# One level of Strassen's algorithm for the base product of batch 1 in a fused cross-attention and LoRA feed-forward kernel

## The reference

```python
q1 = fake_quant(layernorm(x), x1_scale, x1_zp)      # 2 x 1024 x 2048
q2 = fake_quant(ctx, x2_scale, x2_zp)               # 2 x 2048 x 2048
x = x + q1 @ q2                                     # below: x2
n = layernorm(x)
logits = n @ W_router.T                             # 8 experts, two best, softmax weights w
h = einsum('td,erd->ter', n, lora_A)                # rank 16
lora = einsum('ter,eor,te->to', h, lora_B, w) * 2.0
x = x + n @ W_base.T + b_base + lora
```

## Time and profile before

| | |
|---|---|
| median of 3 runs | 1072.69 us (1072.56 to 1073.93) |
| the profiled execution | 1072.88 us |
| its span | 1070.9 us |
| mean granted TensorE clock | 0.99 |
| x2 stage, about | 46 to 308 us |
| routing, about | 308 to 359 us |
| base stage | 359 us to the end |
| moved by DMA | 125.48 MB |

### The profile page before, as it was taken

One profiled execution on the slowest core, in us unless ns is written; L12 is line 12 of the kernel. 1 busy time (PEld: TensorE's weight loads), 2 busy tenths in 40 slices (PEclk: granted clock), 3 DMA queues, 4 the chain that ended last, 5 costly groups with the idle time before them and its releaser, 6 DMA issues.

```text
span 1070.9 us, 15600 instructions
## 1 busy us (share of the span) xinstructions
PE 1011.0 (94%) x6039; PEld 542.3 (51%) x6039; DVE 721.6 (67%) x1334; ACT 311.5 (29%) x284; POOL 18.7 (2%) x40
## 2 busy tenths in 40 slices
PE   0497999899999999999999999999999999999997
PEld 0355666566689644444444444444444444444443
DVE  6758898688756886665665756657566584665744
ACT  3769988778641200010100100101001010010100
POOL 0000000000000000000000000000000000000000
PEclk9899999999999999999999999999999999999999
DMA  7728777476432213123031230321303212132100
GB/s 305 314 111 313 251 243 254 145 253 217 148 128 61 69 64 116 43 93 111 25 105 56 79 110 25 115 68 57 110 24 115 98 37 100 25 115 100 34 20 30
DMA packets 35377, 125.48 MB, mean 117 GB/s; under 512 B 5208, under 2 KB 7304, under 8 KB 29064
## 3 DMA queue, kind: packets, MB, share of 16 engines
q1 hardware_dynamic: 33480, 122.80, 32.1%
q0 software_dynamic: 1280, 2.12, 1.8%
q10 hardware_dynamic: 576, 0.00, 0.0%
HBM read 108.08 MB, written 16.82 MB: 117 GB/s over the span
## 4 chain that ended last, share of the span: by engine, by line
PE 85%; ACT 5%; DVE 5%; issue 3%; DMA 1%; ACTq 0%; DVEq 0%
PE pair L1173 62%; PE pair L1042 14%; PE pair L1147 4%; PE pair L1181 4%; DVE stats L533 2%; ACT ctx_u L430 2%; ACT xt L436 1%; ACT q1T L421 1%; ACT q1u L413 1%; DVE xt L605 1%; ACT pair L450 1%; DMA par<-in_z 1%; DMA rows<-in_x 0%; ACT x2p L444 0%; DVE acc L624 0%
## 5 line engine op out<-in xcount | busy, mean ns | idle before, releaser
L1173 PE MATMUL pair<-x2p,w_p 128*128 128x512 f16 x3072 | 673.5, 379 | 0.0
L1173 PEld LDWEIGHTS pair<-x2p,w_p 128*128 128x128 f16 x3072 | 300.6, 98 | 361.9
L1042 PE MATMUL pair<-q1T,ctx_q 128*128 128x342 f16 x1536 | 236.3, 315 | 0.0
L1042 PEld LDWEIGHTS pair<-q1T,ctx_q 128*128 128x128 f16 x1536 | 150.6, 99 | 77.8
L954 DVE TENSOR_SCALAR sq<-pair,wsc,hsc 128x512 f32<-128x512 f32 x64 | 51.8, 810 | 203.9 <-PE pair L1181 203.9
L493 ACT ACTIVATE w_r<-w_r 128x1024 f32<-128x1024 f32 x32 | 33.8, 1057 | 436.7 <-DVE wst L769 436.7
L500 ACT ACTIVATE w_p<-w_f,wsc 128x1024 f16<-128x1024 f32 x32 | 35.0, 1140 | 153.4 <-issue 120.2
L430 ACT ACTIVATE ctx_u<-ctx_f,par 128x2048 uint8<-128x2048 f32 x32 | 66.6, 2080 | 1.4 <-DVE ctx_q L590 1.4
L605 DVE SCALAR_TENSOR_TENSOR xt<-pair,par,xt 128x342 f32<-128x342 f32 (+1 forms) x96 | 54.4, 567 | 11.8 <-PE pair L1042 11.5
L1022 PE MATMUL pair<-ident,q1w 128*128 128x128 f16 x128 | 11.8, 247 | 47.7 <-ACT q1u L413 30.1
L611 DVE SCALAR_TENSOR_TENSOR x2p<-xt,xs,x2p 128x1024 f16<-128x1024 f32 x32 | 41.0, 1283 | 19.4 <-ACT x2p L444 19.3
(11 more groups left out here) (161 smaller groups left out, 522.4 us busy)
## 6 DMA issues: line engine op xcount, KB each, us to landing
ctx_f<-in_ctx SPq DMA_DIRECT2D x32, 1024.0 KB, 7.4
rows<-in_x SPq DMA_DIRECT2D x16, 1024.0 KB, 9.1
xt<-in_xT SPq DMA_DIRECT2D x32, 512.0 KB, 4.3
w_r<-in_w_n SPq DMA_DIRECT2D x32, 512.0 KB, 4.6
w_f<-in_w_t SPq DMA_DIRECT2D x32, 512.0 KB, 6.5
outT<-u SPq DMA_DIRECT2D x64, 256.0 KB, 2.4
spread<-scratch POOLq DMA_DIRECT2D x16, 128.0 KB, 3.7
ar_f<-in_ar SPq DMA_DIRECT2D x1, 1088.0 KB, 7.8
```

What stands on the lines that cost most here:

```text
L1042: ins = M.matmul(bank[at % RING][:, 0:W3], ctx_q[n % NQ][:, k, :], q1T[b][:, k, c * W3:(c + 1) * W3], start=(k == 0), stop=(k == KT - 1))
L1173: M.matmul(dst, w_p[slot][wh][:, k, :], x2p[b][:, k, xh, t], start=(k == 0 and q == 0), stop=(k == KT - 1 and q == 2))
```

## The change

Batch 0 keeps its 32 outputs, now in order of j with two chunks each (`plain_tile`). Batch 1 becomes 8 units (i = 0 to 7). A unit is the row tiles i and i + 8 by both token halves: four outputs, called quarters. Each of them was a sum of two half products over 1024 features, eight in all; Strassen's algorithm (in Winograd's form) makes them from seven half products of 24 matmuls. For that W's quarters are added and subtracted (`quarter_sum`) and split anew (`s_high` on ScalarE, `s_low` on VectorE, into ten slots), and the products are added up (`take`, seven per unit, one copy on ScalarE, `p1_copy`). The corresponding sums of x2 are made on VectorE during tiles 2 to 9 of batch 0 (`xd_of`, `xd_high`, `xd_low`), kept in memory (`xd_kept`) and loaded over `x2p[0]` when batch 0 is through.

x2 in fp32 is stored to memory from the x2 stage (`keep_x`, 32 x 512 KB) and read back per output straight into `u` (`load_x`, 64 x 256 KB), so that the output group has five instructions on VectorE for seven; the LoRA part's scaling moves to ScalarE (`lora_of`). `w_r` has one buffer for both halves. W is loaded a second time for batch 1 (`load_wq`). The rows of the statistics are held for one batch at a time (`rows_in`). There is no hardware loop any more. The diff, cut to its core:

```diff
--- before.py
+++ after.py
+UNITS = JT // 2
+PRODUCTS = 7
+HOLES = 4
+W_SLOTS = 10
+PLAIN = NC * JT
...
+MADE = [(0, 0, 1), (1, 1, 1), (4, 2, 4), (2, 2, 4), (3, 0, 4), (5, 1, 1), (6, 3, 4)]
+SUMS = (2, 3, 4, 5)
...
+TAKES = 7
+QUARTER_AT = [0, 3, 5, 6]
+FREED = [0, 1, 2, 3, 5, 6, 7]
...
+                    sp.wait_ge(x_stored[n % 3], 16 * (n // 3))
...
+            def keep_x(n):
+                sp.wait_ge(col_added, n + 1)
+                sp.dma_start(x_kept[n, :, :], xt[n % 3][:, :]).then_inc(x_stored[n % 3], 16)
             for n in range(3, STEPS):
+                keep_x(n - 3)
                 load_xt(n)
                 if n + 3 < STEPS:
                     load_ctx(n + 3)
                 if n % 2 and (n + 1) // 2 < TT:
                     load_rows(TT + (n + 1) // 2)
...
+            def load_wr(j, s):
+                if 2 * j + s:
+                    sp.wait_ge(w_summed, 2 * j + s)
+                sp.dma_start(w_r[:, :], w_n[j * P:(j + 1) * P, s * (D // 2):(s + 1) * (D // 2)]).then_inc(wr_landed, 16)
...
+            def rows_in(b):
                 sp.wait_ge(nat_out, 16 * (b + 1))
+                if b:
+                    sp.wait_ge(u_ready, PLAIN)
                 for m, dst in enumerate((rstdB, meanB, shiftB)):
-                    sp.dma_start(dst[:, b * TOKENS:(b + 1) * TOKENS],
-                                 nat_rows[b, m:m + 1, :].to_broadcast([P, TOKENS])).then_inc(spread_landed[b], 16)
...
+            def load_x(m):
+                b, j, c = out_at(m)
+                if m >= 4:
+                    sp.wait_ge(stored[m % 4], 16 * (m // 4))
+                sp.dma_start(u[m % 4][:, :], x_kept[b * JT + j, :, c * CH:(c + 1) * CH]).then_inc(xr_landed[m % 4], 16)
...
+            def load_xd(k):
+                if k:
+                    sp.wait_ge(xd_lo, 2 * k)
+                else:
+                    sp.wait_ge(h_turned, 2 * NC)
+                    sp.wait_ge(h_spread, 2)
+                    sp.wait_ge(nat_out, 32)
+                    sp.wait_ge(hw_ready, 2)
+                for s in range(2):
+                    sp.dma_start(xd[s][:, :], x_kept[JT + k + UNITS * s, :, :]).then_inc(xd_landed, 16)
...
+            for j in range(1, JT):
+                if j + 2 < JT:
+                    load_b(j + 2)
+                    load_wr(j + 2, 0)
+                    load_wf(j + 2)
+                if 2 <= j < 2 + UNITS:
+                    load_xd(j - 2)
+                if j + 2 < JT:
+                    load_wr(j + 2, 1)
+                store(2 * j - 1)
+                load_x(2 * j + 2)
+                load_x(2 * j + 3)
+                if 2 <= j < 2 + UNITS:
+                    store_xd(j - 2)
+                if j == 3 + UNITS:
+                    for s in (0, 1, 2, 3):
+                        load_wq(0, s)
+                store(2 * j)
+                if j == JT - 1:
+                    load_b2(0)
...
+            for s in (0, 2, 1, 3):
+                load_wq(1, s)
+            for s, (k0, half) in enumerate(((0, first), (HALF, second), (0, second), (HALF, first))):
+                sp.wait_ge(g_ready, PLAIN - 1 if half == first else PLAIN)
+                for h in range(2):
+                    sp.dma_start(x2p[0][:, k0:k0 + HALF, h, half],
+                                 xd_kept[k0:k0 + HALF, :, h, half].rearrange("j p t -> p j t")).then_inc(xd_back[s], 16)
+            load_x(PLAIN + 2)
+            rows_in(1)
+            for i in range(UNITS):
+                m = PLAIN + 4 * i
+                store(m - 1)
+                load_x(m + 3)
+                store(m)
+                if i + 1 < UNITS:
+                    load_x(m + 4)
+                    load_b2(i + 1)
+                if i + 2 < UNITS:
+                    load_wq(i + 2, 0)
+                store(m + 1)
+                if i + 1 < UNITS:
+                    load_x(m + 5)
+                if i + 2 < UNITS:
+                    load_wq(i + 2, 2)
+                    load_wq(i + 2, 1)
+                    load_wq(i + 2, 3)
+                store(m + 2)
+                if i + 1 < UNITS:
+                    load_x(m + 6)
+            store(OUTS - 1)
+            for s in range(4):
+                sp.wait_ge(stored[s], 16 * (OUTS // 4))
 
         @block.scalar
...
+            def lora_of(m):
+                act.wait_ge(g_ready, m + 1)
+                if m >= 2:
+                    act.wait_ge(u_ready, m - 1)
...
+            def s_high(i, k):
+                p, s, by = MADE[k]
+                g = PRODUCTS * i + p
+                act.wait_ge(us_ready, i + 1)
+                if k in SUMS:
+                    act.wait_ge(wq_sum, 4 * i + SUMS.index(k) + 1)
+                else:
+                    act.wait_ge(wq_landed[s], 16 * (i + 1))
...
+            w_high(1)
+            lora_of(0)
+            w_sums(2)
+            for j in range(1, JT):
+                if j + 1 < JT:
+                    w_high(j + 1)
+                lora_of(2 * j - 1)
+                if j + 2 < JT:
+                    w_sums(j + 2)
+                if 2 <= j < 2 + UNITS:
+                    xd_high(j - 2)
+                if j == JT - 2:
+                    for k in range(4):
+                        s_high(0, k)
+                if j == JT - 1:
+                    for k in range(4, PRODUCTS):
+                        s_high(0, k)
+                lora_of(2 * j)
+            lora_of(PLAIN - 1)
...
+            def out_of(m, src, by):
+                b, j, c = out_at(m)
                 t = slice(c * CH, (c + 1) * CH)
-                src = x2p[b][:, bass.ds(j, 1), :, cc * CH:(cc + 1) * CH]
-                if stored_at is not None:
-                    dve.wait_ge(stored[c], stored_at)
...
+                V.scalar_tensor_tensor(o[:, :], meanB[:, t], wsum[:, j:j + 1], o[:, :], ALU.mult, ALU.add).then_inc(u_step, 1)
+                dve.wait_ge(u_step, 2 * m + 1)
+                V.tensor_tensor(o[:, :], o[:, :], shiftB[:, t], ALU.add).then_inc(u_step, 1)
+                dve.wait_ge(lora_taken, m + 1)
+                V.scalar_tensor_tensor(s[:, :], src[:, :], by, s[:, :], ALU.mult, ALU.add).then_inc(g_taken, 1)
+                dve.wait_ge(g_taken, m + 1)
+                V.tensor_tensor(s[:, :], s[:, :], rstdB[:, t], ALU.mult).then_inc(g_step, 1)
+                dve.wait_ge(g_step, m + 1)
+                dve.wait_ge(u_step, 2 * m + 2)
+                V.scalar_tensor_tensor(o[:, :], s[:, :], bias_s[:, j:j + 1], o[:, :], ALU.add, ALU.add).then_inc(u_ready, 1)
...
+            def xd_low(k):
+                for s in range(2):
+                    dve.wait_ge(xd_hi, 2 * k + s + 1)
+                    V.scalar_tensor_tensor(xd_p[s][:, 1, :], xd[s][:, :], xsT[:, 0:1], xd_p[s][:, 0, :], ALU.mult, ALU.subtract).then_inc(xd_lo, 1)
...
+            def make(i, k):
+                if k in SUMS:
+                    quarter_sum(i, k)
+                s_low(i, k)
...
+            def take(i, k):
+                dst, one, p = ((ct, p1c, 1), (u2, p1c, 2), (u3, u2, 3), (ct, u3, 4), (u2, u2, 4), (ct, u2, 5), (ct, u3, 6))[k]
+                dve.wait_ge(product, PRODUCTS * i + p + 1)
+                if k == 0:
+                    dve.wait_ge(p1_copied, i + 1)
+                if TAKES * i + k:
+                    dve.wait_ge(c_taken, TAKES * i + k)
+                if k in QUARTER_AT:
+                    dve.wait_ge(g_taken, PLAIN + 4 * i + QUARTER_AT.index(k))
+                V.tensor_tensor(dst[:, :], one[:, :], product_bank(i, p)[:, :], ALU.add).then_inc(c_taken, 1)
...
+            w_max_of(2, 0)
+            plain_out(0)
+            w_max_of(2, 1)
+            w_bound_of(2)
+            for j in range(1, JT):
+                if j + 1 < JT:
+                    w_scale_of(j + 1)
+                    lora_scale_of(j + 1)
+                    w_low(j + 1)
+                if j + 2 < JT:
+                    w_max_of(j + 2, 0)
+                plain_out(2 * j - 1)
+                if 2 <= j < 2 + UNITS:
+                    xd_of(j - 2)
+                if j + 2 < JT:
+                    w_max_of(j + 2, 1)
+                    w_bound_of(j + 2)
+                if 2 <= j < 2 + UNITS:
+                    xd_low(j - 2)
+                if j == JT - 2:
+                    unit_scale(0)
+                    for k in range(4):
+                        make(0, k)
+                if j == JT - 1:
+                    for k in range(4, PRODUCTS):
+                        make(0, k)
+                plain_out(2 * j)
...
+            b2_of(0)
+            for i in range(UNITS):
+                more = i + 1 < UNITS
+                if more:
+                    unit_scale(i + 1)
+                if i:
+                    quarter_out(i - 1, 3)
+                else:
+                    plain_out(PLAIN - 1)
+                if more:
+                    make(i + 1, 0)
+                    make(i + 1, 1)
+                quarter_out(i, 0)
+                if more:
+                    make(i + 1, 2)
```

(73 more changed lines are left out.)

500 lines of the change are left out of this document (323 added, 177 removed).

## The result

The changed kernel takes 1155.6 us (median of 4 runs, 1154.4 to 1158.5), the kernel before 1072.8 us beside it: a ratio of 1.077 [1.075, 1.080]. It is slower, as forecast, but by 83 us where 11 were forecast, and the time lies outside the range of 1050 to 1112. A DMA is a transfer to or from memory; its landing is the moment at which the profile shows it complete.

The account below looks back on a forecast made before the run. TensorE alone was taken to bound the base stage. From 1072.9 us, batch 0's loop added 21, starting up 5.6, the x2 stage 0, and batch 1 with its change-over took off 15.2, giving 1084.3; range 1050 to 1112.

Parts of the forecast that it names:

- The x2 stage: Storing x2 per chunk on SyncE's queue was to be hidden by the chunks' products: cost 0, ends 0 and +6.
- 300 GB/s of the forecast: In the x2 stage, the added stores were to raise memory traffic from 245 to some 300 GB/s.
- Batch 0: Weight preparation in tiles with xd becomes a 24.5 us loop against TensorE's 22.0: cost 21 us, ends 9 and 33.
- a loop without xd: Batch 0's preparation in tiles without xd: 20.6 us, below TensorE's 22.0, so no cost.
- Starting up: First w_r halves load serially, delaying routing and tile 4 by 2.8 us each: 5.6 us, ends 0 and 12.
- The change-over: Between batches, batch 1's rows queue behind x2's sums, so VectorE's first output starts 41.3 us after batch 0's last tile.
- VectorE's lateness: At the end of batch 0, VectorE was to finish 4.5 us after tile 31.
- The units: In batch 1, VectorE needs 40.1 us per unit against TensorE's 38.9; with the change-over, gain 15.2, not 41.5.
- The fourth: Rival: x2 stage loses 6 us, xd's small pieces run at half speed, loop is 26; 1117 us, chance 0.12.
- The first: Rival: later transfers don't wait for earlier ones, so xd and batch 1's rows land sooner; 1061 us, chance 0.17.
- third: Rival: transfers queue but take 3.2 us alone and 1.2 behind another, loop 23.1; 1067 us, chance 0.06.
- The second: Rival: all preparation stays hidden and the full 41.5 us from fewer matmuls are gained; 1033 us, chance 0.03.

Follow-up runs that it names:

- Experiment 1: The kernel before plus only the x2 store (32 of 512 KB) from SyncE's queue, ahead of the next xt load: 1129.6 us, ratio 1.053.
- 2 and 3: Two edits, each alone on the changed kernel: x2 stores issued on GpSimd's queue, 1112.9 us; context load issued ahead of the xt load, 1119.6 us.
- experiment 11: e9 with another change-over order, plus first maximum, w_r's second load and the sum of row sums moved in batch 0's loop: 1043.2 us, ratio 0.9722.
- e6: Changed kernel with x2 stores and batch 1's rows on GpSimd's queue, xd loads before w_f, and ScalarE's even-output copy ahead of high halves: 1090.4 us.
- e9: Changed kernel with GpSimd x2 stores and rows, early xd loads, plus reordered batch 0 preparation and unit 0's weights from row tile 12: 1058.7 us.
- e7: e6 with loads of x2's sums on GpSimd's queue, lora_B's ahead of the last store, and batch 1's rows back on SyncE's queue: 1085.9 us.
- e2: Changed kernel with the context load issued ahead of the xt load on SyncE's queue in the x2 stage: 1119.6 us, ratio 1.043.
- e1: Changed kernel with the x2 stores issued from GpSimd's queue in place of SyncE's: 1112.9 us, ratio 1.037.

## Why the prediction was right or wrong

**The x2 stage: the step that failed.** It said of the store that "xt's slot comes back 2 to 3 us later, with two chunks of slack", cost 0, ends 0 and +6. The stage lost 39.4. The share and bandwidth of rows 2 were the wrong rows for it. What decides is the order of issues: the store of chunk n-3 stands directly ahead of the load of xt n, which waits for that store's landing, and directly behind a context load of 1 MB. There is no slack of two chunks in that order: the queue waits for a landing of its own last issue, once per tile, and the tile takes that landing and 0.9 of issues. Experiment 1 shows the store alone to be enough, and 2 and 3 that neither bytes nor bandwidth are the cause. With the store on another queue the stage loses 2.2 (310.6 for 308.3), inside the ends that I gave, and moves the 300 GB/s of the forecast. So its bandwidth was right and its waiting wrong. Of the 71 us by which the forecast missed, this step has 39; batch 0 has 22, the change-over and the units together 9, routing 2.

**Batch 0.** Forecast 23.8, measured 45.3. The mechanism was right for the tiles with xd. From the scale to xd's subtraction I gave 12.0; the eight periods show 13.6, as a load of xd lands 7.0 us after its issue in the median (6.1 to 8.5), where the sum had 5.1 for the first and 6.1 for the second. From there to the next scale I gave 12.5; measured 26.05 - 13.56 = 12.49. So the loop is 26.05 for 24.5, at the upper end given. TensorE's tiles 6 to 22 take 26.3 a period (210.2 us), so 34.0 over TensorE's 22.0 for a forecast of 21. Of these, 23.4 are waits and 10.7 are matmuls at a lower clock; as TensorE follows VectorE's loop there, the lower clock takes the place of waiting and isn't a cost of its own. One term was missing: tiles 22 to 31 lost 6.6 where a loop without xd was to cost nothing. The four periods of VectorE there take 24.0, 25.6, 23.4 and 21.7 us, for 20.6 in the sum, and the last tiles wait for ScalarE's copy behind unit 0's high halves. The 20.6 used a round trip of 9.4; its own rows give 605.65 - 595.86 = 9.8, too little to matter.

**Starting up.** Forecast 5.6: 2.8 for routing, measured 4.5, and 2.8 for tile 4. Tile 6 starts 71.7 after tile 0, where before two more tiles behind rows 8 make 67.2: 4.5. The wait was right, 2.87 us; the rest is the clock, to which the sum gave nothing:

```profile
450.50:452.00 1.50, 1.49 (x4) 0.54 (x5) 1.50 (x2) 0.00 (x0) 0.00 (x0) 0.50 0.51 161
...
451.77 11.45 PE L1596 MATMUL pair<-x2p,w_p 128*128 128x512 f16 x48
```

Behind the wait the granted clock is 0.50, the lower of the two levels, and the 3 small and 48 large matmuls take 1.6 us more than the 0.81 and 10.52 elsewhere. Right in kind, 3.4 too low together.

**The change-over.** The first output was forecast at 41.3 after tile 31, measured 48.8. VectorE's lateness (output 30's store is issued 8.5 after tile 31, 4.5 forecast) is 4.0 of the 7.5. The rest is 3.5: counting the transfers by their bytes was nearly right. Each load of x2's sums holds SyncE for 2.9 us, the time that 1 MB takes in the sum too (2 x 1.45), with the DMA engines at a share of 1.05. And TensorE's stall ahead of its third product, which the sum let VectorE's wait cover, is 11.3, with 8.3 more in unit 1 for lora_B's halves, which no step named.

**The units.** VectorE's 40.1 was too high. TensorE has no idle in the window of batch 1 above, at 38.85 a unit (907.81 to 946.66), with VectorE busy 83%. This error went the other way and hid part of the one before, by luck: together -6.5 for -15.2.

**The rivals.** The fourth had the right places (x2 stage, xd's pieces, a loop of 26), but its 6 us for the first is 39. The first and third fell: transfers do queue, and xd landed later than the sum had it, not earlier. By the figures of the Trainium skill named there ("DMA: Bandwidth & Descriptors", section "Anatomy of one DMA"), 3.2 us for 512 KB is the estimate, and it would have made all of it cheaper still: the x2 stores take 2.6 us at best, but 7.9 in the median. The section gives its figures for transfers that GpSimd issues; those of this sum are SyncE's. The second, that all stays hidden, was closest to what the kernel of experiment 11 does: 1043 for 1033.

## What to carry to other kernels

When a DMA is added to an in-order queue, don't ask first what bandwidth it takes, but what is behind it: write down the queue's order for one period, with each wait, and see whether an issue waits for the landing of one just ahead of it. When work is added to a loop of several engines, move whole steps under the longest round trip and look which engine is idle in the new period; moving one late link gained nothing (e6, 6 us lost). Covering the round trip, together with an earlier start on the next stage's weights, was worth 26 us (e9), but the period itself became shorter only when the waits that took its place were filled too (e11, 12 us more).

## What was unexpected of the hardware

Eight loads of 1 MB in a row (x2's sums, in runs of 1 KB) take SyncE 2.9 us each to issue in the median (817 to 3376 ns), where 512 KB loads take 0.33 to 0.43 in the x2 stage, and land 10.3 to 12.8 us after. The 256 KB load behind them takes 2.92 as well. The DMA engines move 341 GB/s at a share of 1.05 meanwhile, so a full queue explains it as well as the short runs; no run tells the two apart. From GpSimd's queue (e7) the same loads take 0.88 each to issue.

A store of 512 KB takes 2.6 to 10.0 us to land in the changed kernel: 7.9 in the median behind a 1 MB load, 5.9 behind a 512 KB one (e2), and on GpSimd's queue 6.5 (e1), but 4.5 to 6.6 in the later runs with the same stores.

After TensorE's 11.3 us of idle ahead of its third product, the 48 matmuls at 827.03 take 13.22 us for 10.52, at a granted clock of 0.79. For shorter waits the length alone doesn't tell: after 2.28 us of waiting (until 619.66) the next 48 take 12.21, after 2.91 us (until 646.45) they take 10.52:

```profile
620.32 12.21 PE L1596 MATMUL pair<-x2p,w_p 128*128 128x512 f16 x48
...
647.11 10.52 PE L1596 MATMUL pair<-x2p,w_p 128*128 128x512 f16 x48
```
